# First attention: start beside the projections' last stores, earlier query loads, five query places

## The reference

```
q, k = x @ Wq_sem.T | rope(x @ Wq_geo.T), the same for k      # 16 heads of 32
v = x @ Wv.T
scores = (q @ k.T) * 32 ** -0.5, causal
attn = softmax(scores)
out = (attn @ v) @ Wo.T
x = layernorm(x + out)
```

## Time and profile before

| what | us |
|---|---|
| median of three runs | 2338.95 (2334.89 to 2340.2) |
| profiled execution | 2335.38 |
| its span, first to last instruction | 2333.6 |
| mean granted TensorE clock | 0.971 |

### The profile page before, as it was taken

The page is one execution under the profiler, slowest core; times in us unless marked ns, Lnnn a source line. Parts: engine busy times, 40 slices in busy tenths (PEclk is TensorE's granted clock), DMA queues, the critical chain, the costliest instruction groups (busy, mean ns, idle before and its releaser), DMA issues. The chain is left out here.

```text
span 2333.6 us, 27534 instructions
## 1 busy us (share of the span) xinstructions
PE 2186.3 (94%) x10140; PEld 1507.2 (65%) x10140; DVE 1191.6 (51%) x2311; ACT 746.6 (32%) x1334; POOL 675.0 (29%) x461
## 2 busy tenths in 40 slices
PE   7978999999999789999979899999998999999996
PEld 5865555555554354444447787888887887878775
DVE  6764677676663363222236752232326546554665
ACT  3322455555556332111134431121123211212122
POOL 5333455555556313252222350000003021212100
PEclk9986899999999899999999999999999999999998
DMA  4564444442320335565543362000101010100001
GB/s 172 192 172 119 110 120 119 120 106 55 72 52 20 98 147 192 161 132 93 92 100 126 119 218 89 19 28 19 32 14 55 1 37 19 36 18 27 10 19 54
DMA packets 104363, 197.25 MB, mean 85 GB/s; under 512 B 10272, under 2 KB 27552, under 8 KB 102816
## 3 DMA queue, kind: packets, MB, share of 16 engines
q1 hardware_dynamic: 91968, 162.78, 23.8%
q0 software_dynamic: 11408, 29.69, 5.7%
q10 hardware_dynamic: 864, 3.15, 0.4%
HBM read 123.82 MB, written 71.75 MB: 84 GB/s over the span
## 5 line engine op out<-in xcount | busy, mean ns | idle before, releaser
L626 ACT ACTIVATE a_probs<-a_stb 128x512 f32<-128x512 f32 (+3 forms) x640 | 308.8, 534 | 272.2 <-PE a_stb L738 158.6
L594 POOL TENSOR_TENSOR a_probs<-a_probs 128x1024 f32<-128x1024 f32 (+3 forms) x160 | 282.0, 1774 | 276.0 <-PE a_avb L750 261.5
L652 DVE TENSOR_REDUCE a_mparts<-a_sbank 128x1 f32<-128x512 f32 x384 | 239.8, 683 | 101.0 <-PE a_sbank L712 100.8
L2102 POOL CAST m_wh<-wst 128x1024 fp32r<-128x1024 f32 x24 | 27.6, 1148 | 723.8 <-POOLq L1429 369.0
L57 PE MATMUL m_gu<-hi,m_wh 128*128 128x512 f32 x512 | 202.4, 395 | 14.5 <-DVE m_h L2168 13.1
L58 PE MATMUL m_gu<-lo,m_wh 128*128 128x512 f32 x512 | 201.2, 393 | 0.0
L59 PE MATMUL m_gu<-hi,m_wl 128*128 128x512 f32 x512 | 201.0, 393 | 0.0
L712 PE MATMUL a_sbank<-hi,q 96*128 96x512 f32 (+3 forms) x320 | 134.0, 448 | 24.0 <-PEq L153 12.6
L750 PE MATMUL a_avb<-a_probs,V 128*32 128x512 f32 (+3 forms) x1280 | 153.5, 552 | 0.7 <-ACT a_probs L626 0.7
L657 DVE CUSTOM_DVE_ANT_0 a_junk<-a_sbank,hidden 128x128 bf16<-128x128 f32 (+3 forms) x256 | 113.3, 488 | 71.3 <-PE a_sbank L712 69.8
L2168 DVE TENSOR_TENSOR m_h<-m_sg,m_gu 128x512 f32<-128x512 f32 x64 | 44.0, 687 | 206.0 <-ACT m_sg L2132 205.9
(11 more groups left out here) (268 smaller groups left out, 4763.6 us busy)
## 6 DMA issues: line engine op xcount, KB each, us to landing
qk<-v_hl SPq DMA_DIRECT2D x32, 512.0 KB, 2.9
hi<-qk SPq DMA_DIRECT2D x60, 256.0 KB, 5.4
lo<-qk SPq DMA_DIRECT2D x60, 256.0 KB, 6.2
q<-qk SPq DMA_DIRECT2D x48, 256.0 KB, 5.6
wst<-in_w_mlp SPq DMA_DIRECT2D x24, 512.0 KB, 3.5
xs<-a_zeros POOLq DMA_DIRECT2D x39, 264.0 KB, 2.8
X<-xs SPq DMA_DIRECT2D x39, 264.0 KB, 2.7
v<-vhl SPq DMA_DIRECT2D x16, 512.0 KB, 4.6
```

Source lines behind the costliest of these rows:

```text
L594: nc.gpsimd.tensor_tensor(probs[:, i % PSLOTS, hs, w0:], probs[:, i % PSLOTS, hs, w0:], probs[:, (i + 1) % PSLOTS, hs, w0:], ALU.add)\
L626: nc.scalar.activation(probs[:, i % PSLOTS, h, w0:], stb[:, k % 3, w0:], ACT.Exp, scale=SCALE0)\
L652: nc.vector.reduce_max(to, sbank[:, b, :], AX).then_inc(s["unit_max"], 1)
```

## The change

- In the last chunk of the projections the list becomes qk(12), qk(13), v(12), qk(14), qk(15), v(13), v(14), v(15).
- The six early query loads are issued a chunk sooner, behind the stores of ("qk", 2, 3), k = 11; the six key loads stay where they were. Each item has a semaphore for its six loads, on which TensorE waits before the item's first unit.
- The waits at the end of the projections' SP list leave. The one for the stores is now the first thing in SP's list of the attention. `hl` is the first buffer that is allocated, so that it lies under `probs`, which is written only after that wait.
- The projections' semaphores aren't cleared at the attention's start but together with the attention's own, a stage later.
- Queries have five places while n < 8: 0 to 4 by n % 5, from item 8 on 0 to 2 by (n - 8) % 3. The two new places `qx` are the memory of `X[:, 8:16]`, which outputs of items 8 and later use. The planner and SP wait for the item that had the place before: none for items 3 and 4, item 0, 1, 2 for items 5, 6, 7, and n - 3 from item 8 on, as before.

```diff
+INX = 2
+def query_slots(items):
+    slot = [n % (QSLOTS + INX) if n < 2 * NG else (n - 2 * NG) % QSLOTS for n in range(items)]
+    old = [max((o for o in range(n) if slot[o] == slot[n]), default=-1) for n in range(items)]
+    return slot, old
...
         def chunk(c):
             ev = [("qk", c, 0), ("qk", c, 1), ("v", c, 0), ("qk", c, 2)]
-            ev += [("x", c + 1, 0)] * (c + 1 < NC)
-            return ev + [("v", c, 1), ("qk", c, 3), ("v", c, 2), ("v", c, 3)]
+            if c + 1 < NC:
+                return ev + [("x", c + 1, 0), ("v", c, 1), ("qk", c, 3), ("v", c, 2), ("v", c, 3)]
+            return ev + [("qk", c, 3), ("v", c, 1), ("v", c, 2), ("v", c, 3)]
...
-                    if c == NC - 1 and j == 1:
+                    if c == NC - 2 and j == NG - 1:
                         for n in range(EARLY):
                             sp.wait_ge(hstore[n], 16)
                             sp.wait_ge(lstore[n], 16)
-                            for dst, src in (*queries_in(qk_dram, n, 0, qst[:, n]),
-                                             *keys_in(qk_dram, n, 0, kst[n])):
-                                sp.dma_start(dst, src).then_inc(s["early"], 16)
-            sp.wait_ge(s["early"], 16 * 6 * EARLY)
-            for store in (*hstore, *lstore):
-                sp.wait_ge(store, 16 * NC * NG // 2)
+                            for dst, src in queries_in(qk_dram, n, 0, qst[:, n]):
+                                sp.dma_start(dst, src).then_inc(s[f"early{n}"], 16)
+                    if c == NC - 1 and j == 1:
+                        for n in range(EARLY):
+                            for dst, src in keys_in(qk_dram, n, 0, kst[n]):
+                                sp.dma_start(dst, src).then_inc(s[f"early{n}"], 16)
...
-            free = max(freed[n, unit[2]], final[n - QSLOTS] if n >= QSLOTS else -1)
+            free = max(freed[n, unit[2]], final[q_old[n]] if q_old[n] >= 0 else -1)
...
-        stage_before.give_back()
+        m.sems += stage_before.sems
...
+            for store in stored:
+                sp.wait_ge(store, 16 * NC * NG // 2)
             work, queries = [], -1
...
-                    after = final[n - QSLOTS] if n >= QSLOTS else -1
+                    after = final[q_old[n]] if q_old[n] >= 0 else -1
...
+                    if n < EARLY and j == 0:
+                        pe.wait_ge(landed[n], 16 * 6)
...
+        qx = nc.alloc_sbuf_tensor_at("qx0", [P, INX, GH, CH], F32R, offset=floor + 4 * (NT - INX * TC) * D)
```

More of the change, by code:

```diff
@@ L155, in layer0_qkv @@
         hidden, ident, identr, maskr = consts
+        hl = m.sb("hl", [P, 2, 2, 2, CH], F32R)
         maskf = m.sb("maskf", [P, P])
@@ L162, in layer0_qkv @@
         rotated = m.sb("rotated", [P, 2, CH])
-        hl = m.sb("hl", [P, 2, 2, 2, CH], F32R)
         xh, xl = (a[:, 0:2, :].rearrange("p b (d n) -> p b d n", d=ND) for a in (hi, lo))
@@ L172, in layer0_qkv @@
         names = ("w0 w1 w2 x0 x1 cs0 cs1 xhi xlo whi_a wlo_d whi_p wlo_p qk_ok qkf_ok v_ok vs_ok rot_ok "
-                 "t1_ok sin_ok sum_ok hi_ok lo_ok hstore0 hstore1 lstore0 lstore1 consts early").split()
+                 "t1_ok sin_ok sum_ok hi_ok lo_ok hstore0 hstore1 lstore0 lstore1 consts early0 early1").split()
         s = {k: m.sem(k) for k in names}
@@ L372, in _ @@
             pe.wait_ge(s["vs_ok"], NT)
-    return m
+    return m, (*hstore, *lstore), (s["early0"], s["early1"])
 def attention0_plan():
@@ L406, in attention0_plan @@
     lead = 7500.0
+    q_old = query_slots(len(items))[1]
     loads, last_use = [], {}
@@ L476, in attention0_plan, with layer0_attention @@
     return items, steps, first, final, units, loads, last_use, order
-def layer0_attention(nc, stage_before, qk_dram, m_dram, xs_dram, acc_dram, token, V, X, hi, lo, qst, consts, early):
+def layer0_attention(nc, stage_before, stored, landed, qx, qk_dram, m_dram, xs_dram, acc_dram, token, V, X, hi, lo, qst, consts, early):
     items, steps, first, final, units, loads, last_use, order = attention0_plan()
@@ L492, in layer0_attention @@
     NI = len(items)
+    q_slot, q_old = query_slots(NI)
+    q_loads = [len([o for o in range(EARLY, n + 1) if q_slot[o] == q_slot[n]]) for n in range(NI)]
     with ExitStack() as ctx:
@@ L497, in layer0_attention @@
         kst = key_slots(hi, lo)
+        qs = [qst[:, i] for i in range(QSLOTS)] + [qx[:, i] for i in range(INX)]
         probs = m.sb("probs", [P, PSLOTS, GH, CH])
@@ L516, in layer0_attention @@
         kload = [m.sem(f"kload{i}") for i in range(KSLOTS)]
-        qload = [m.sem(f"qload{i}") for i in range(QSLOTS)]
+        qload = [m.sem(f"qload{i}") for i in range(QSLOTS + INX)]
         mrow = (s["mrow0"], s["mrow1"])
-        stage_before.give_back()
+        m.sems += stage_before.sems
         block = ctx.enter_context(nc.Block())
@@ L533, in q_in @@
                     sp.wait_ge(s["st_ok"], 4 * (after + 1))
-                for dst, src in queries_in(qk_dram, items[n][1], items[n][0], qst[:, n % QSLOTS]):
-                    sp.dma_start(dst, src).then_inc(qload[n % QSLOTS], 16)
+                for dst, src in queries_in(qk_dram, items[n][1], items[n][0], qs[q_slot[n]]):
+                    sp.dma_start(dst, src).then_inc(qload[q_slot[n]], 16)
             def max_in(n):
@@ L540, in max_in @@
                 sp.wait_ge(s["mstore"], 16 * (n + 1))
-                sp.dma_start(f32(qst[96:97, n % QSLOTS]).rearrange("o h n -> o (h n)"),
+                sp.dma_start(f32(qs[q_slot[n]][96:97]).rearrange("o h n -> o (h n)"),
                              m_dram[n].rearrange("r q -> (r q)").unsqueeze(0)).then_inc(mrow[n % 2], 16)
+            for store in stored:
+                sp.wait_ge(store, 16 * NC * NG // 2)
             work, queries = [], -1
@@ L703, in _ @@
                     at = slot_of[n, u]
+                    if n < EARLY and j == 0:
+                        pe.wait_ge(landed[n], 16 * 6)
                     if n not in fresh_q:
                         fresh_q.add(n)
-                        pe.wait_ge(qload[n % QSLOTS], 48 * (n // QSLOTS + (n % QSLOTS >= EARLY)))
+                        pe.wait_ge(qload[q_slot[n]], 48 * q_loads[n])
                     if at not in fresh_k:
@@ L711, in _ @@
                     bank = free(ev)
-                    nc.tensor.matmul(bank[:, 0:w], qst[0:96, n % QSLOTS, h, t * P:(t + 1) * P],
+                    nc.tensor.matmul(bank[:, 0:w], qs[q_slot[n]][0:96, h, t * P:(t + 1) * P],
                                      kst[at % KSLOTS][0:96, h, 0:w], start=True, stop=True)\
@@ L735, in _ @@
                         kst[slot_of[n, kt // TC] % KSLOTS][0:97, h, kt % TC * P:(kt % TC + 1) * P],
-                        qst[0:97, n % QSLOTS, h, w0:], start=True, stop=kt < TC * c)
+                        qs[q_slot[n]][0:97, h, w0:], start=True, stop=kt < TC * c)
                     if kt >= TC * c:
@@ L2270, in build @@
         slot_a, slot_b = (ctx.enter_context(nc.sbuf_tensor(f"slot_{k}", [P, NT], mybir.dt.int32)) for k in "ab")
+        floor = (nc.sbuf_base + 31) // 32 * 32
         X = ctx.enter_context(nc.sbuf_tensor("X", [P, NT, D], F32))
+        qx = nc.alloc_sbuf_tensor_at("qx0", [P, INX, GH, CH], F32R, offset=floor + 4 * (NT - INX * TC) * D)
         ident1 = ctx.enter_context(nc.sbuf_tensor("ident1", [P, P], F32))
@@ L2306, in build @@
                 consts = (hidden, ident, identr, maskr)
-                stage = layer0_qkv(nc, ins["xT"], ins["wqk0"], ins["wv0"], ins["rope0"], ins["masks"], ins["eye"],
+                stage, stored, landed = layer0_qkv(nc, ins["xT"], ins["wqk0"], ins["wv0"], ins["rope0"], ins["masks"], ins["eye"],
                                    X, V, hi, lo, qst, consts, qk0_dram)
-                stage = layer0_attention(nc, stage, qk0_dram, m_dram, xs_dram, acc_dram, ins["token"], V, X, hi, lo, qst, consts, early)
+                stage = layer0_attention(nc, stage, stored, landed, qx, qk0_dram, m_dram, xs_dram, acc_dram, ins["token"], V, X, hi, lo, qst, consts, early)
             xt = V[:].rearrange("p (d c) n -> p d (c n)", d=ND)
```

## The result

| | before | after |
|---|---|---|
| median, us | 2339.57 (4 runs, 2334.89 to 2344.64) | 2299.39 (4 runs, 2298.76 to 2307.89) |
| profiled execution, us | 2335.38 | 2298.76 |
| ratio | | 0.9838, 95% interval 0.9812 to 0.9865 |

The kernel became 1.6% faster, 1.35 to 1.88% by the interval. Two later jobs (a job is a set of runs taken together, with runs of the kernel before among them) gave the changed kernel 0.985 (0.983 to 0.9869; median 2302.57) and 0.9839 (0.9818 to 0.9861; median 2302.42).

The account below looks back on a forecast made before the run. TensorE was taken to bound the attention only from about 282 us on. Gains 5.5 + 28 = 33.5 us take the profiled 2335.38 to 2301.9; the median lies 3.6 higher, so 2305, range 2296 to 2322.

Parts of the forecast that it names:

- The wait before v(15): Last projection chunk: TensorE waits 4.5 us for ScalarE's eviction of v(13), so the first unit starts at 156.5 to 159.4.
- Stores and loads: Projections' end: sooner query loads cost 0, last stores land near 156, and neither block's end nor TensorE waits for them.
- Items 0 to 3: First attention's early stretches, priced by item at 18.0, 12.9, 13.8 and 12.4 us, plus 16.1 for item 4's first half.
- The cross-check: Same attention stretches priced as 482 matmuls at 0.169 us: 81.7 us, a gain of 22.
- Queues: SP's list in the attention: nine loads, 10.2 us of queue, stand before the small maxima store; cost taken 0.
- The slower rival: First scores of items 1 to 5 wait for late maxima rows and the clock halves; 2347 us, chance 0.03.
- the oscillating clock: TensorE's clock goes to and fro in items 1 to 3, costing 11.6 us; 2317 (2312 to 2324), chance 0.21.
- Less than it says: Another engine holds items 1 to 3 at their old pace; gain 5.5 + 0 to 10, 2323 to 2334, chance 0.09.
- nothing given back: Attention from step 13 on: list, loads and waits unchanged and TensorE the bound, so the gain stays.
- the change of stage: From projections to attention: first unit matmul sooner than 163.32, gain 6.8 to 3.9 us, taken as 5.5.
- items 0 to 4: First attention's early stretches: 73.2 us against 103.8, gain taken as 28, ends 20 and 33.

Follow-up runs that it names:

- e4: Changed kernel, but ScalarE evicts v(13) and v(14) before waiting for the sum of k=15; medians 2304.14 and 2301.53 us in two jobs.
- e5: Changed kernel with all twelve early loads at their old place in the last chunk, no wait at the block's end; 2306.16 us, ratio 0.987.
- e7: Changed kernel with one wait put back: SP holds the query loads of item 5 until step 11; 2310.16 us, changed kernel 2302.42 in that job.
- e8: Changed kernel plus an unread 512-column matmul behind each of the 32 units of items 0 and 1; 2300.36 us, ratio 0.9841.
- e9: Changed kernel with the extra matmuls of e8 and the sooner evictions of e4 together; 2301.1 us, ratio 0.9831.
- after_third: Third profile of the changed kernel, nothing altered, run again as its job's reference; median 2302.42 us, profiled execution 2300.78 us.
- e3: Changed kernel with five query places, but the planner's list as before, units in lumps at steps 5 and 9; 2309.69 us, ratio 0.9871.

## Why the prediction was right, and where its sizes were off

The prediction was 2305 in 2296 to 2322; measured 2299.39, 2302.57 and 2302.42.

- **The wait before v(15)**: 4.5 us predicted, 4.29 measured; it held the block's end, as e4 showed by removing it. First unit predicted at 156.5 to 159.4, measured 158.86, and 158.15 and 160.10 in the two later profiles, the last outside; the gain I took, 5.5 us, was 4.5 (3.2 to 5.2 by the three). v(15) took 4.61 us (153.05 to 157.66, its clock at half for part), nearer to the upper bound than I took.
- **Stores and loads**: SP's drain at 154.2 was out of the way, as said. The issue of the six query loads took 4.03 us, as two times the 1.93 us of the earlier trace rows would have said, and not some 3; it held nobody. The sooner query loads I costed at nothing whichever way; e5 shows that without them 1.2 us would be lost, at a place that I hadn't looked at: the row of item 0's maxima behind the loads of item 2.
- **Items 0 to 3**: this was the sum's main term and it held. Predicted 18.0, 12.9, 13.8, 12.4 and 16.1; measured 18.03, 13.37, 15.27, 12.36 and 16.13. In all 75.2 against 73.2, and a gain of 28.6 against the 28 taken. It rests on the clock's return some 10 us after the first scores, as before; in the second profile of the changed kernel the return was late and steps 0 to 8 alone took 9.1 us more. Item 2 is 1.5 us over, its 21 units being held up by VectorE (waits of 0.3 and 1.0 us, 11.66 us busy of 15.27). The cross-check by the mean price of a matmul (0.169 us) was the worse estimate: items 1 to 3 came to 0.13 to 0.15 us a matmul.
- **Queues**: SP waited up to 10.1 us for a maxima store to land (25.8 us in five waits, 8.3 the longest before), the 10.2 us that nine loads were to cost: the store issued at 200.05 stands behind nine of them. The row was in time for every item. The slower rival failed by this slack.

```profile
SPq L554 <- DMA max<-a_msb: 25.8, 5, 10.1
```

- **The clock**: in the first profile it came back 8.6 us after the first exp and stayed. I gave the oscillating clock 0.21 as if it were a property of the kernel. It is one of the execution: in the three profiles of the changed kernel it came back 8.6, 32 and 9.2 us after the first exp, and in e4 again after 20 us. Between the first and the second that is 9.1 us in steps 0 to 7. In the Trainium skill, "TensorE: Matmul & The Clock Gate", section "What's actually happening", the return is called variable between runs; these profiles agree. Of the page's section "A second HAM failure mode: psum-queue depth-cycling" in the Trainium skill, by which short idles between groups make the clock go to and fro, this case shows little: the kernel turns through three banks and stayed at 1.00 from 183.87 to 747.06 in the first and from 185.6 to 745.4 in the third profile, and fell once in between, at 339.9, in the second.
- **Less than it says, nothing given back**: the lead of 33.4 us at step 20 was 33.5 at the end of the attention in the first profile. In the second, 4.7 us went at the later fall of the clock.
- **What was mis-sized**: the whole, by 3.1 us in the profiled execution (36.6 instead of 33.5). The terms up to the attention's end give 33.5 and are right in sum, partly since their misses offset: the change of stage was taken 0.8 to 1.0 us too high and items 0 to 4 0.6 us too low; the rest came behind the attention, where I had taken 0. The changed kernel's own three profiles differ by as much there: the last den starts at 744.74, 757.93 and 746.22, and the executions take 2298.76, 2317.08 and 2300.78, so behind the attention the second is 5.1 us longer than the first and the third 0.5. From the last exp to the end of the span it is 1558.9 us in the kernel before, 1555.8 in the changed one, and 1555.3 to 1564.7 in the other twelve profiles, so 3.1 us is less than executions differ there. Against a predicted 2305 the medians of 2299.39 to 2302.57 are closer than the spread of single executions (2298.58 to 2317.08) lets one claim for the method.

## What to carry to other kernels

Where an engine's list was planned around a scarce buffer, more places can pay twice: the wait goes, and the work piled up behind it can be spread between other work. Here 12.6 us of waits were 17.3 us with their slow clock and 28.6 with the spreading. Price the new list per stage, by the engine that bounds it, from rows of like work at the same clock; that sum was within 2.0 us in 75. When a step is moved ahead in one order for all engines, look at what each of them evicts or frees behind it: the last chunk's reordering was to gain the rotation 0.3 us, and put a wait of 4.3 us on TensorE.

## What the runs showed of the hardware that was not expected

- In a wait of TensorE of 4.90 us the clock fell 2.9 us after the wait began and stayed at half for 10.24 us; in all the wait cost 8.6 us (e7).
- The clock's return differs between executions of one program: 8.6 to 32 us after the first exp, 30.0 to 39.1 us for the same 187 matmuls. With 32 matmuls that filled idle time it was full from 156.5 on, before the first scores, and the 187 took 26.65 us (e8); with the same 32 it fell once more in e9, from 172.5 to 179.4.
- The clock fell to half for 10.24 us in a stretch that TensorE was busy from end to end (10.24 of 10.24 us, second profile of the changed kernel). It did so in three of the profiles, at 337.2, 339.9 and 358.6, the same place of the program, and for 3.4 us in a fourth, at 339.7. Each time TensorE had waited 1.14 or 1.15 us for VectorE just before, and the fall came 0.6 to 1.4 us after that wait ended. The same wait of 1.14 or 1.15 us, without a fall, is in the profiles of before, after, after_third, e3 and e8, so it can't be the whole cause; what else it takes no run here shows.
- The experts' scatters, 38 in a row, can be a chain of their own: in one profile of 14 (the first of e4) 30 of them from 990 us on waited for the landing of the one before, and TensorE waited 10.28 us at the stage's end instead of 5.6 to 6.0, which took back 4.4 us of a lead from the stages before.
